# First loads in another order, no constant-tile matmuls behind the first transposes, and a new set of queue preferences in a causal attention and top-k FFN block

## The reference

```python
def attn(x):                                   # B, T, C = 2, 4096, 256
    q, k, v = jnp.split(x @ w_attn + b_attn, 3, axis=-1)
    mask = where(tril(ones((T, T))), 0.0, -1e10)
    a = softmax(einsum('btc,bsc->bts', q, k) / sqrt(C) + mask)
    return einsum('bts,bsc->btc', a, v) @ w_proj + b_proj

def ffn(x):                                    # k = int(0.75 * T) = 3072
    scores = einsum('bld,d->bl', x, w_router)
    _, top = top_k(scores, k)
    return x.at[rows, top].set(gelu(x[top] @ w_block))

x = layernorm(x + attn(x))
out = layernorm(x + ffn(x))
```

## Time and profile before

| | |
|---|---|
| Median of 3 runs | 954.26 us (953.89 to 955.04) |
| Span of the profiled execution | 953.7 us |
| PE busy | 931.6 us (98%) |
| DVE busy | 785.4 us (82%) |
| ACT busy | 633.7 us (66%) |
| POOL busy | 305.0 us (32%) |
| DMA | 155.84 MB, mean 163 GB/s |
| Chain that ended last | PE 85%, DVE 7%, ACT 4%, issue 2%, DMA 1% |

### The profile page before, as it was taken

How to read it: one execution, slowest core, us unless ns; L and a number is a source line. 1 busy time by engine, 2 the same in 40 slices (tenths; PEclk the granted TensorE clock), 3 DMA queues, 4 the chain that set the end, 5 groups by cost and what they waited for, 6 DMA issues and landing times.

```text
span 953.7 us, 15684 instructions
## 1 busy us (share of the span) xinstructions
PE 931.6 (98%) x5030; PEld 798.6 (84%) x5030; DVE 785.4 (82%) x1497; ACT 633.7 (66%) x1011; POOL 305.0 (32%) x460
## 2 busy tenths in 40 slices
PE   9999999999999999999999999999999999999992
PEld 6889998888888888888888999888888888888871
DVE  5898887866994896589879999998699799659977
ACT  3576665864774594479565866677578569547994
POOL 3541141242230335333325361452022244301243
PEclk9999999999999999999999999999999999999996
DMA  6644344344353355468634534346777734437934
GB/s 193 206 123 154 104 144 122 103 144 152 101 185 113 111 155 175 146 205 263 195 104 149 189 93 142 130 123 207 234 238 226 242 113 134 150 105 238 323 124 177
DMA packets 89044, 155.84 MB, mean 163 GB/s; under 512 B 8442, under 2 KB 18300, under 8 KB 88964
## 3 DMA queue, kind: packets, MB, share of 16 engines
q1 hardware_dynamic: 88964, 154.85, 51.0%
HBM read 114.96 MB, written 39.86 MB: 162 GB/s over the span
## 4 chain that ended last, share of the span: by engine, by line
PE 85%; DVE 7%; ACT 4%; issue 2%; DMA 1%; DVEq 0%; SPq 0%; ACTq 0%
PE sbank L587 37%; PE fbank L587 12%; PE obank L1236 9%; PE obank L1237 9%; PE obank L1238 9%; PE obank L1232 2%; PE obank L1230 2%; PE obank L1231 2%; DVE ring L1147 1%; ACT parts L1161 1%; DVE ring_lo L1166 1%; ACT ring L1154 1%; DMA ring<-xt 1%; DVE tail L2037 1%; PE mbank L1134 1%
## 5 line engine op out<-in xcount | busy, mean ns | idle before, releaser
L587 PE MATMUL sbank<-qT,xT 128*128 128x512 f32 (+2 forms) x1728 | 406.6, 377 | 1.1 <-ACT ring L1021 1.0
L587 PEld LDWEIGHTS sbank<-qT,xT 128*128 128x128 f32 x1728 | 306.4, 188 | 54.9 <-ACT ring L1021 1.1
L1021 ACT COPY ring<-sbank 128x512 f32<-128x512 f32 (+3 forms) x286 | 157.2, 553 | 178.3 <-PE sbank L587 125.1
L1166 DVE TENSOR_TENSOR ring_lo<-ring,parts 128x1024 fp32r<-128x1024 f32 (+4 forms) x174 | 181.1, 1050 | 32.2 <-ACT parts L1161 31.4
L1161 ACT CAST parts<-ring 128x1024 fp32r<-128x1024 f32 (+4 forms) x174 | 145.0, 843 | 48.1 <-PE obank L1238 34.1
L1070 DVE TENSOR_TENSOR runmax<-ring,runmax 128x1024 f32<-128x1024 f32 x84 | 107.1, 1274 | 69.0 <-ACT ring L1021 68.1
L1147 DVE TENSOR_TENSOR ring<-ring,mbank 128x1024 f32<-128x1024 f32 (+4 forms) x174 | 157.0, 955 | 5.6 <-PE mbank L1134 5.3
L1236 PE MATMUL obank<-ring_lo,vs 128*128 128x512 f32 (+3 forms) x416 | 158.9, 382 | 0.2 <-DVE ring_lo L1166 0.2
L1238 PE MATMUL obank<-parts,vs 128*128 128x512 f32 (+3 forms) x416 | 157.4, 378 | 0.0
L1237 PE MATMUL obank<-parts,vs 128*128 128x512 f32 (+3 forms) x416 | 157.4, 378 | 0.0
L1154 ACT ACTIVATE ring<-ring 128x1024 f32<-128x1024 f32 (+4 forms) x174 | 142.2, 852 | 9.7 <-DVE ring L1147 9.5
(11 more groups left out here) (268 smaller groups left out, 1371.4 us busy)
## 6 DMA issues: line engine op xcount, KB each, us to landing
vs<-v_scratch SPq DMA_DIRECT2D x288, 256.0 KB, 2.9
v_scratch<-vnew SPq DMA_DIRECT2D x30, 512.0 KB, 3.5
out<-tail SPq DMA_DIRECT2D x32, 256.0 KB, 2.6
xres<-x SPq DMA_DIRECT2D x15, 512.0 KB, 3.9
x_scratch<-xres SPq DMA_DIRECT2D x14, 512.0 KB, 3.9
y_scratch<-yb SPq DMA_DIRECT2D x14, 512.0 KB, 3.0
tail<-x_scratch SPq DMA_DIRECT2D x28, 256.0 KB, 3.6
tail<-y_scratch SPq DMA_DIRECT2D x28, 256.0 KB, 4.3
```

The costliest lines, as they stand in the source:

```text
L587: mm = eng.matmul(o, lhs(lh, k), rhs(rh, k), start=n == 0, stop=n == len(todo) - 1)
L1021: act.copy(slot(n)[:, c0:], sbank[n % NSS][:, c0:]).then_inc(a_copy, 1)
L1166: dve.tensor_tensor(slots_lo(ns, c0), slots(ns, c0), f32(hi_of(u)), ALU.subtract).then_inc(v_lo, 1)
```

## The change

The waits and streams of the first loads are set anew: the value weights no longer wait for x; x transposed for groups 1 and 2 is put in the stream "prepare", directly behind the projection bias and without a wait; the block weights and the router row get streams and semaphores of their own and wait for x of group 1 and of group 2; the residual rows of the first two groups wait for x of group 2. `block_sums` gets a PE stream of its own, "prepare block", in place of its place behind the scores of the fourth tile. HELD is 0. All values of `PREFER_US`, `MARGIN_US`, `BEFORE_LAST_US` and `LAST_US` are replaced; the cost table is not touched.

```diff
-HELD = 3
+HELD = 0
...
-PREFER_US = {"final result": 2182, "scores copy": 1183, "prepare keys": 1153, "final pick": 1052,
...
+PREFER_US = {"final result": 7363, "attention_out evac": 5500, "ffn flo": 5170, "final scale": 5004,
...
-MARGIN_US = {"late": 8, "project xhi": 8, "prepare bias": 8, "final_roots": 8, "attention_out store": 8,
...
+MARGIN_US = {"attention_out store": 24.2, "final pick": 14.3, "late": 13.1, "project xhi": 11.2, "final own": 10.2,
...
+        ld_wr = sem("ld_wr")
...
             def load_w(sp):
-
-
-                sp.wait_ge(ld_xh[0], 16)
                 sp.dma_start(wv_t, wt_rows[2]).then_inc(ld_wv, 16)
                 sp.dma_start(wp, w_proj.rearrange("(k p) c -> p k c", p=P)).then_inc(ld_w, 16)
                 sp.dma_start(bp_row, b_proj.rearrange("(a c) -> a c", a=1)).then_inc(ld_w, 16)
 
             def load_block(sp):
+                sp.wait_ge(ld_xt0[1], 16)
                 sp.dma_start(wb, w_block.rearrange("(k p) c -> p k c", p=P)).then_inc(ld_ffw, 16)
-                sp.dma_start(wr[:, :], w_router.rearrange("(a c) -> a c", a=1).broadcast_to([P, C])).then_inc(ld_ffw, 16)
+
+            def load_router(sp):
+                sp.wait_ge(ld_xt0[2], 16)
+                sp.dma_start(wr[:, :], w_router.rearrange("(a c) -> a c", a=1).broadcast_to([P, C])).then_inc(ld_wr, 16)
...
             at("sp", "prepare", load_w)
-            at("sp", "prepare", load_block)
...
-                pe.wait_ge(ld_ffw, 32)
+                pe.wait_ge(ld_ffw, 16)
...
-            behind_scores.extend([[lambda pe: query_sums(pe, 0)], [lambda pe: query_sums(pe, 1), bias_product], [bias], [block_sums]])
+            behind_scores.extend([[lambda pe: query_sums(pe, 0)], [lambda pe: query_sums(pe, 1), bias_product], [bias]])
+            at("pe", "prepare block", block_sums)
...
-                dve.wait_ge(ld_ffw, 32)
+                dve.wait_ge(ld_wr, 16)
                 dve.tensor_reduce(sum_w[:, :], wr[:, :], AX.X, ALU.add).then_inc(v_sw, 1)
...
+            for n in range(1, EARLY + 1):
+                project_load(n)
+            at("sp", "prepare block", load_block)
+            at("sp", "prepare router", load_router)
...
             def load(sp):
-                if G <= EARLY:
-                    sp.wait_ge(ld_wv, 16)
                 if G == EARLY + 1:
                     xlo_made(sp, 0)
...
-            at("sp", "project load", load)
+            at("sp", "prepare" if G <= EARLY else "project load", load)
...
                 else:
-                    sp.wait_ge(ld_wv, 16)
+                    sp.wait_ge(ld_xt0[2], 16)
                 sp.dma_start(r, x_rows[b][:, tile0:tile0 + QT, :]).then_inc(ld_x[G % 2], 16)
...
-            if G:
+            if G > EARLY:
                 project_load(G)
```

More of the change, by code:

```diff
@@ new lines @@
+PREFER_US = {"final result": 7363, "attention_out evac": 5500, "ffn flo": 5170, "final scale": 5004,
+             "project qlo": 5000, "prepare late": 4446, "row_max reduce": 4000, "scores copy": 3499,
+             "attention_out ot": 3371, "ffn fhi": 3268, "ffn scale": 3212, "project load": 3068, "project vhi": 2994,
+             "attention_out aggr": 2698, "attention_out load": 2641, "attention_out score": 2565, "project vlo": 2283,
+             "project xhi": 2205, "ffn add": 2202, "late load": 2149, "search": 1795, "prepare block": 1648,
+             "search first": 1128, "last": 989, "project qhi": 894, "last chain": 832, "softmax lo": 746,
+             "prepare router": 620, "attention_out norm": 590, "softmax z": 426, "prepare bias": 394, "row_max": 316,
+             "softmax hi": 128, "softmax exp": -13, "attention_out istd": -163, "late": -199, "final_roots own": -212,
+             "scores running": -432, "attention_out residual": -460, "final choose": -478, "attention_out stats": -690,
+             "attention_out router": -801, "project vstore": -822, "bias columns": -1004, "final pick": -1033,
+             "last router": -1216, "final load": -1441, "values load": -1477, "ffn stats": -1656, "scores hide": -1688,
+             "project xlo": -1782, "final store": -1795, "ffn sums": -1932, "prepare": -2213, "ffn aggr": -2216,
+             "prepare xlo": -2323, "ffn gelu": -2466, "prepare keys": -2497, "final sums": -2643, "final own": -3593,
+             "attention_out store": -3904, "ffn store": -5311, "final_roots": -5972, "ffn rows": -10430}
@@ new lines @@
+LAST_US = {"out": 7071, "final sums": 5871, "final scale": 5408, "attention_out evac": 4795, "row_max": 4602,
+           "ffn store": 4311, "ffn add": 4250, "attention_out router": 3938, "ffn rows": 3815, "search": 3600,
+           "bias columns": 3391, "values load": 3308, "attention_out store": 3180, "final choose": 2964,
+           "ffn aggr": 2908, "prepare late": 2677, "attention_out aggr": 2122, "final load": 1478, "scores hide": 1390,
+           "final pick": 1320, "prepare router": 1267, "prepare xlo": 1183, "attention_out norm": 1181,
+           "project qhi": 867, "attention_out residual": 769, "softmax lo": 465, "project vhi": 447,
+           "attention_out ot": 440, "search first": 386, "values": 312, "ffn stats": 287, "ffn scale": 219,
+           "softmax z": 187, "scores": 176, "attention_out load": 167, "final_roots": 14, "attention_out score": -4,
+           "proj": -19, "prepare block": -49, "scores running": -182, "prepare": -202, "ffn flo": -306,
+           "final_roots own": -334, "final result": -621, "final store": -765, "attention_out stats": -804,
+           "project xhi": -881, "softmax hi": -890, "late load": -1295, "last router": -1455, "softmax exp": -1663,
+           "row_max reduce": -2131, "final own": -2353, "ffn fhi": -2586, "prepare bias": -2924, "ffn sums": -3066,
+           "scores copy": -3492, "ffn gelu": -3938, "project xlo": -4293, "project qlo": -4312, "last chain": -4319,
+           "project vlo": -4455, "late": -4701, "project vstore": -5327, "last": -5552, "attention_out istd": -5711,
+           "project load": -6114, "prepare keys": -8648}
@@ L800, in block_parts @@
             def block_parts(dve):
-                dve.wait_ge(ld_ffw, 32)
+                dve.wait_ge(ld_ffw, 16)
                 dve.wait_ge(p_wsum, 1)
```

26 lines of the change are left out of this document (added).

## The result

The changed kernel takes 967.51 us (median, 966.37 to 967.78), the kernel before, run beside it, 954.57 (953.89 to 955.04). The ratio is 1.0132, with a 95% interval of 1.012 to 1.0145: it is 13 us slower, where I forecast 3 us faster and a range that ended at 955.3.

A forecast was written before the change was run, and what follows sets the result against it. TensorE was taken as the bound, busy for 931.6 of 953.7 us. The terms gave 953.7 - 1.30 - 1.10 - 0.67 = 950.6 us of span, with 0.56 added 951.2 us; range 948.8 to 955.3.

The forecast's parts named there:

- The middle at zero: 60 to 900 us: new preferences change nothing for TensorE; bounds 0.87 us gained, 1.5 us lost.
- my own sign of being right: 60 to 900 us: less than 1.5 us of TensorE holes would show the forecast right.
- The preferences: All five queues ordered anew: zero taken for 60 to 900 us, 0.67 us won after it.
- The constant tiles: Behind the first and second transposes: two batches of constant matmuls hid nothing, so 2 x 0.65 = 1.30 us go.
- The front: First loads: earlier xt removes the 1.00 us scores-copy wait and half of a 0.17 us wait, together 1.10 us.
- the second rival: Start: another wait takes over the gain of the first loads, only 1.30 us stays, 953.0 us; chance 0.13.
- the danger of more bytes beside it: First loads: 512 KB of weights in flight with x could delay it; taken as nothing, bound 1.5 us.
- The tail: Search rounds and ACT's last copy: 0.67 us won, between 2.9 us won and 4.6 us lost.
- the rival of ACT's order: ACT, 900 to 930 us: work put ahead of the chain costs up to 4.6 us, 956.5 us, slower; chance 0.17.
- The clock: First transposes: a longer TensorE hole without constant matmuls halves the clock, costing 1.8 us, 953.7 us; chance 0.05.
- From span to run: Whole kernel: the median of runs stands 0.56 us above the profiled span, added to the forecast span.
- the rival that the latter names: Tail in a better order: search not held up, ACT's copy first, 2.9 us won, 949.0 us; chance 0.20.

## Why the prediction was wrong

**The middle at zero, at most 1.5 us lost, is the step that failed.** I argued from shares: DVE and ACT not full, PE hardly waiting, so a new order has reserve, and I bounded the loss by nine waits of the size seen. It measured 7.5 us of new holes (8.36 in all, where my own sign of being right was less than 1.5), and 2.8 us of low clock behind the largest. The reserve of an in-order queue is not its idle time; it is how early each item stands before what it waits for. SP never shows as busy, and I read only its front. Its wait for output stores, 15.4 us in the kernel before, was in the trace and is the row that I missed: two buffers, a store's landing and a load in one queue with the v blocks. By its longest wait there, 3.9 us, I would have had a bound above the 1.5 that I took. The runs show both halves: the new tables alone bring 1.0135, and the SP order alone, put into before, 1.0143, some of it by a second hole of its own. SP's order isn't all of it, though: with the loads later again 1.0077 stays, and what ACT's own new order has in that was not separated. The Trainium skill (DMA: Bandwidth & Descriptors, "Anatomy of one DMA — SWDGE (gpsimd) path") states that DMA engines don't wait for semaphores, the issuing sequencer does, before it dispatches; the trace agrees for SP's queue, where from 682.44 to 687.42 nothing is issued.

**The preferences as one term.** I took the new tables as one cause and the loads and constant tiles as edits whose orders stay put. The old tables on the other two edits cost 4.8 us, while the same edits in the old order cost nothing (ratio 0.998). These edits made the planner choose anew, and that had a price of its own, which my sum had nowhere.

**The constant tiles** (1.30 of span): right; 0.93 in the runs, 0.2 to 2.9 by the interval.

**The front** (1.10): the steps came as foretold. SP issues xt for group 1 at 4.63 (forecast near 4.5), ACT converts it at 10.67 (before 11), no scores copy holds PE before 20 us. But the gain was taken over, as the second rival had it, by a wait that I hadn't named:

```profile
10.67 1.05 ACT L881 CAST xT<-ring 128x1024 fp32r<-128x1024 f32 x1 [3.27 <-DMA ring<-xt]
11.62 1.26 ACT L937 ACTIVATE qT<-fbank,ucol 128x512 fp32r<-128x512 f32 x2
...
13.85 1.62 PE L589 MATMUL sbank<-qT,xT 128*128 128x512 f32 x6 [1.22 <-ACT qT L937]
```

The new order puts the conversion, still waiting for its load, ahead of ACT's part of the queries, and PE waits 1.22 us for these. The term was also read from one execution. The kernel without the constant tiles has the old loads, and in its profile 15 to 20 us has no hole: its xt was converted at 14.66 and not at 15.98. The 1.00 us was at least in part how the loads happened to land. (I also had the scores matmuls through 1.5 us before their copy; they were over at 14.26, 2.7 us before it.) Its window, and the conversion in its timeline:

```profile
15.00:20.00 5.00, 5.00 (x33) 1.00 0.94 320
```

```profile
14.66 1.05 ACT L876 CAST xT<-ring 128x1024 fp32r<-128x1024 f32 x1 [2.63 <-DMA ring<-xt]
```

x itself was converted at 6.08 against 5.91, so the danger of more bytes beside it was 0.17 us.

**The tail** (0.67 gained): 0.5 lost, within the bounds. The rounds of the search that I read in the earlier trace rows as 3.06, 1.76 and 2.43 us are 3.15, 1.76 and 2.37 (they start at 937.72, 940.87, 942.63 and 945.00): the new order kept the long one, so the 0.67 was hope for a better choice and no reading. PE's holes grew from 18.97 to 19.5 us. ACT's table loads fell from 30 to 28, so the rival of ACT's order gave nothing, though its sign and a loss of its kind (a queued item ahead of what PE needs) were right, 200 us earlier than I looked.

**The clock** fell before 930, which I had given 0.05 and placed at the first transposes. The place was the one large hole that the order made, and the price 2.8 us against 1.8. That a loss of this kind came at all was luck: it was foreseen for another place and another cause. The rows that I held against it were of one execution. In the profile of the kernel before without its first output, whose front is that of before, a hole of 0.57 us ended at 17.26, and the granted clock was 0.77 in 17 to 18, 0.50 in 18 to 20 and 0.53 in 20 to 21.

**From span to run** I added 0.56. The profile of the changed kernel is its fastest run, and its span lies 3.2 us under the median; 2.3 of the 13 us are the growth of this gap (3.2 less 0.9). Of the range, 949.9 and the lower end, 948.8, have no working; the rival that the latter names is 949.0.

## What to carry to other kernels

An idle engine is not slack. Before a planned order is changed, look in the waits of the issuing queue for buffers whose release goes through a store's landing, and ask what stands behind each such wait; where two buffers turn over through memory, in a queue that also carries what the bounding engine needs, the distance between store and next load is a quantity to protect. And when an order is made anew, freeze the old one and apply the edits one by one: here the part without the new order won 0.2%, and with it the kernel lost 1.3%.

## What was not expected of the hardware

The landing of one 256 KB store is not a constant: its median was 2.7 us in one order and 4.2 to 4.3 in two others, with the same bytes, the longest wait in the chain being 5.47. With the 5.25 us hole filled, one of 2.33 us was followed by a granted clock of 0.83 in its window; a hole of 1.00 us in before was granted 1.00, and one of 0.57 us in another execution of that front was followed by 0.50. And the same first load of the second group's x had landed for ACT at 15.98 in one execution and at 14.66 in another.
